# Edge ordering of a four-layer graph network: the one-hots laid down in four sub-blocks of four columns

## The chip, the cores and the metric

The kernel runs on one core of one Trainium2 chip. The metric is the device time of one launch, in microseconds (us), from all inputs in HBM to the output in HBM; lower is better. The engines are TensorE (PE in the profile; PEld is its weight load), VectorE (DVE), ScalarE (ACT), GpSimd (POOL) and SyncE (SP), which only issues transfers here.

## The reference, cut to what matters

Four message-passing layers over 6250 nodes and 200000 edges, with a residual sum and a layer norm after each.

```python
edge_index = jnp.stack([src, dst])
deg = jnp.maximum(jax.ops.segment_sum(jnp.ones(dst.shape, jnp.float32), dst, num_segments=6250), 1.0)
...
x = _layernorm(x + _L0_gnn_ref(x, deg_isqrt[:, None], L0_gnn_weight, L0_gnn_bias, src, dst), axis=-1)
x = _layernorm(x + _L1_gnn_ref(x, L1_gnn_w_neigh, L1_gnn_w_self, L1_gnn_b_self, src, dst), axis=-1)
x = _layernorm(x + _L2_gnn_ref(x, edge_index, L2_gnn_W1, ...), axis=-1)
x = _layernorm(x + _L3_gnn_ref(x, edge_index, L3_gnn_W1, ...), axis=-1)
```

Each layer gathers rows by `src` and sums them by `dst` (or the other way round). The edges come sorted by `dst`; the kernel first sorts them by tile of `src` as well, so that all later stages work on whole 128x128 or 128x512 pieces. The change touches this sorting alone, and nothing of the layers.

## The kernel before, in words

`program` runs its steps one after the other. A step ends with a barrier of all engines, so a step that ends earlier moves all later steps up by as much. `sort_edges` is the first step. It lays the edges down as 98 blocks (`BLOCKS`) of `K` = 16 columns of 128 edges, and has four parts: `load_columns`, `rank_columns` (the place of each edge in its block), `permute_columns` (each edge's record to its place, and the degrees), `bucket_ranges`.

`permute_columns` is where the change lies. For each block `n` (buffer half `h` = `n % 2`), the engines do this:

- VectorE (L386 to L391) makes five fp16 tiles. `lane` compares the 16 columns' lane numbers with a ramp of 64 values: 64x16 = 1024 elements in each partition. `row` does so with 128 values: 2048 elements. `dlo` does it for the last four columns: 128x4 = 512 elements. `piece` is `lane` times the high part and `lane` times the low part of the payload: 1024 elements each. In all of them the column is the innermost index, so the elements of one column are 16 elements, 32 bytes, apart (in `dlo`: four elements, 8 bytes). Before it starts it waits for `s_used`, which TensorE raises at the end of block `n - 2`. After every second block it also makes seven tiles of `high` for the next segment of 14 blocks (L396); in the last segment it doesn't.
- ScalarE (L443) makes `step`, 12 tiles of 128 elements in each partition, one for each of the first twelve columns (`steps(n + 1, ...)`, which waits for `s_used` too), and then takes block `n`'s sums out of PSUM (`results`, L448 and L449), once TensorE has summed them and the transfer of block `n - 2` has landed (`s_put`).
- TensorE sums the 16 columns in PSUM (L478): the stationary operand is `row[:, h, :, k]`, 128 columns wide, the moving one `piece[:, h, :, :, k]`, 128 columns wide, both read with a step of 32 bytes. Then come four matmuls for `dlo` (L481) and twelve for `step` (L484), each with a contiguous or 8-byte stationary operand and a moving operand `high` of 49 columns whose step is 448 bytes. `dlo` and `step` keep their forms under the change, and `high` does.
- GpSimd (L418, L421) adds the two parts and sends 128 records to HBM by an indirect transfer that accumulates.

```python
for k in range(K):
    put = nc.tensor.matmul(ps[:, h, 0:2 * LANES], row[:, h, :, k], piece[:, h, :, :, k].rearrange("p a l -> p (a l)"), start=k == 0, stop=k == K - 1)
put.then_inc(s_full, 1)
for k in range(OWN, K):
    nc.tensor.matmul(psh[:, 0:NT], dlo[:, h, :, k - OWN], tile_of(k), start=False, stop=False)
pe.wait_ge(s_step, n + 1)
for k in range(OWN):
    ins = nc.tensor.matmul(psd[:, 0:NT], step[:, h, k, :], tile_of(k), start=False, stop=False)
ins.then_inc(s_used, 1)
```

Of the kernel before, what the change touches and what calls it, by code (L numbers as in the profile page):

```python
# [5 lines left out]
F16 = mybir.dt.float16  # L6
# [3 lines left out]
ALU = mybir.AluOpType  # L10
# [3 lines left out]
P = 128  # L14
# [3 lines left out]
NT = -(-N_NODES // P)  # L18
# [2 lines left out]
CJ = 13  # L21
SCP = CJ * P
K = 16
LANES = 64
BLOCKS = -(-N_EDGES // (P * K))
CC = BLOCKS * K
# [38 lines left out]
def load_columns(nc, m, src, dst):  # L65
# [5 lines left out]
    with ExitStack() as ctx:  # L71
        sb = lambda n, s, d: ctx.enter_context(nc.sbuf_tensor(n, s, d))
# [24 lines left out]
        @block.gpsimd  # L97
        def _(gp):
            ch = Chain(gp, s_const)
            nc.gpsimd.memset(m.ones[:, :], 1.0).then_inc(s_const, 1)  # L100
            nc.gpsimd.iota(m.iota512[:, :], pattern=[[1, DB]], base=0, channel_multiplier=0, allow_small_or_imprecise_dtypes=True).then_inc(s_const, 1)
            nc.gpsimd.iota(m.iota128[:, :], pattern=[[1, P]], base=0, channel_multiplier=0, allow_small_or_imprecise_dtypes=True).then_inc(s_const, 1)
            nc.gpsimd.iota(m.row_id[:, :], pattern=[[0, 1]], base=0, channel_multiplier=1, allow_small_or_imprecise_dtypes=True).then_inc(s_const, 1)
            nc.gpsimd.iota(m.ramp[:, :, :], pattern=[[1, P], [0, K]], base=0, channel_multiplier=0, allow_small_or_imprecise_dtypes=True).then_inc(s_const, 1)
            ch.n = 5
            ch(nc.gpsimd.memset(m.zeros16[:, :], 0.0))
            ch(nc.gpsimd.affine_select(out=m.ident[:, :], in_=m.ones[:, :], compare_op=ALU.is_equal, fill=0.0, base=0, pattern=[[1, P]], channel_multiplier=-1))
            ch(nc.gpsimd.affine_select(out=m.before[:, :], in_=m.ones[:, :], compare_op=ALU.is_gt, fill=0.0, base=0, pattern=[[1, P]], channel_multiplier=-1))
            ch(nc.gpsimd.affine_select(out=m.shift1[:, :], in_=m.ones[:, :], compare_op=ALU.is_equal, fill=0.0, base=-1, pattern=[[1, P]], channel_multiplier=-1))
            ch(nc.gpsimd.affine_select(out=corner[:, :], in_=m.ones[:, :], compare_op=ALU.is_equal, fill=0.0, base=P - 1, pattern=[[1, P]], channel_multiplier=-1))  # L110
            nc.gpsimd.memset(zero[:, :], 0.0).then_inc(s_zero, 1)
# [229 lines left out]
def permute_columns(nc, m):  # L341


    OWN = 12
    SUB = 14
    SUBS = BLOCKS // SUB
    PAIRS = SUB // 2
    assert SUBS % 2 == 1 and NT % PAIRS == 0
    with ExitStack() as ctx:
        sb = lambda n, s, d: ctx.enter_context(nc.sbuf_tensor(n, s, d))  # L350
        sem = lambda n: nc.alloc_semaphore("pm_" + n)
        lane = sb("lane_hot", [P, 2, LANES, K], F16)
        piece = sb("piece_hot", [P, 2, 2, LANES, K], F16)
        row = sb("row_hot", [P, 2, P, K], F16)
        step = sb("dst_step", [P, 2, OWN, P], F16)
        dlo = sb("dst_low_hot", [P, 2, P, K - OWN], F16)
        high = sb("dst_tile_hot", [P, 2, NT, SUB * K], F16)
# [12 lines left out]

        @block.vector
        def _(dve):
            spread_over = lambda t, c, n, k: t[:, bass.ds(c, k)].unsqueeze(1).broadcast_to([P, n, k])
            for t in range(NT):
                ins = nc.vector.tensor_scalar(high[:, 0, t, :], m.dst_hi[:, 0:SUB * K], float(t), None, ALU.is_equal)
                if t % PAIRS == PAIRS - 1:
                    ins.then_inc(s_high, 1)

            def segment(s, turn, more=True):

                with dve.Fori(0, PAIRS) as i:
                    for h in (0, 1):
                        n = s * SUB + i * 2 + h
                        c = n * K
                        dve.wait_ge(s_used, n + 1)
                        nc.vector.tensor_tensor(lane[:, h, :, :], spread_over(m.lane, c, LANES, K), m.ramp[:, 0:LANES, :], ALU.is_equal).then_inc(s_lane, 1)  # L386
                        nc.vector.tensor_tensor(row[:, h, :, :], spread_over(m.rowkey, c, P, K), m.ramp[:, :, :], ALU.is_equal)
                        nc.vector.tensor_tensor(dlo[:, h, :, :], spread_over(m.dst_lo, c + OWN, P, K - OWN), m.ramp[:, :, 0:K - OWN], ALU.is_equal)
                        dve.wait_ge(s_lane, n + 1)
                        nc.vector.tensor_tensor(piece[:, h, 0, :, :], lane[:, h, :, :], spread_over(m.part1, c, LANES, K), ALU.mult)  # L390
                        nc.vector.tensor_tensor(piece[:, h, 1, :, :], lane[:, h, :, :], spread_over(m.part2, c, LANES, K), ALU.mult).then_inc(s_hot, 1)  # L391

                    if more:
                        for k in range(NT // PAIRS):
                            t = i * (NT // PAIRS) + k
                            ins = nc.vector.tensor_scalar(high[:, 1 - turn, bass.ds(t, 1), :].rearrange("p o w -> p (o w)"), m.dst_hi[:, bass.ds((s + 1) * (SUB * K), SUB * K)],  # L396
                                                          m.iota128[:, bass.ds(t, 1)], None, ALU.is_equal)
                        ins.then_inc(s_high, 1)

            with dve.Fori(0, SUBS // 2) as j:  # L400
                for turn in (0, 1):
                    segment(j * 2 + turn, turn)
            segment(SUBS - 1, 0, more=False)
            ch = Chain(dve, s_v)
            dve.wait_ge(s_counts, 1)

            ch(nc.vector.tensor_copy(si[:, :], psd[:, 0:NT]))
            ch(nc.vector.tensor_scalar(si[:, :], si[:, :], 1023, None, ALU.bitwise_and))
            ch(nc.vector.tensor_copy(sl[:, :], si[:, :]))
            nc.vector.tensor_tensor(sh[:, :], psd[:, 0:NT], sl[:, :], ALU.subtract).then_inc(s_parts, 1)  # L410
            ch(nc.vector.tensor_copy(counted[:, :], psh[:, 0:NT]))
            dve.wait_ge(s_deg, 1)
            ch(nc.vector.tensor_tensor(m.deg[:, :], counted[:, :], psd[:, 128:128 + NT], ALU.add))
# [47 lines left out]
        @block.tensor  # L461
        def _(pe):
            pe.sem_inc(s_used, 2)  # L463
            for p in (psd, psh):
                nc.tensor.matmul(p[:, 0:NT], m.zeros16[:, 0:P], m.zeros16[:, 0:NT], start=True, stop=False)

            def segment(s, turn):

                pe.wait_ge(s_high, (s + 1) * PAIRS)
                pe.sem_inc(s_begun_pe, 1)  # L470
                with pe.Fori(0, PAIRS) as i:
                    for h in (0, 1):
                        n = s * SUB + i * 2 + h
                        tile_of = lambda k: high[:, turn, :, bass.ds(i * (2 * K) + (h * K + k), 1)].rearrange("p t o -> p (t o)")
                        pe.wait_ge(s_both, n + 1)
                        pe.wait_ge(s_hot, n + 1)
                        for k in range(K):
                            put = nc.tensor.matmul(ps[:, h, 0:2 * LANES], row[:, h, :, k], piece[:, h, :, :, k].rearrange("p a l -> p (a l)"), start=k == 0, stop=k == K - 1)  # L478
                        put.then_inc(s_full, 1)
                        for k in range(OWN, K):  # L480
                            nc.tensor.matmul(psh[:, 0:NT], dlo[:, h, :, k - OWN], tile_of(k), start=False, stop=False)  # L481
# [5 lines that stand above are left out]
            with pe.Fori(0, SUBS // 2) as j:  # L487
                for turn in (0, 1):
                    segment(j * 2 + turn, turn)
            segment(SUBS - 1, 0)  # L490
            nc.tensor.matmul(psh[:, 0:8], m.zeros16[:, 0:P], m.zeros16[:, 0:8], start=False, stop=True)
            nc.tensor.matmul(psd[:, 0:8], m.zeros16[:, 0:P], m.zeros16[:, 0:8], start=False, stop=True).then_inc(s_counts, 1)
            pe.wait_ge(s_parts, 1)
            nc.tensor.matmul(psd[:, 128:128 + NT], m.steps[:, :], sl[:, :], start=True, stop=False)
            nc.tensor.matmul(psd[:, 128:128 + NT], m.steps[:, :], sh[:, :], start=False, stop=True).then_inc(s_deg, 1)
# [326 lines left out]
def sort_edges(nc, m, src, dst):  # L822
    with ExitStack() as ctx:
# [7 lines left out]
        m.before16 = sb("before16", [P, P], F16)  # L831
        m.shift1 = sb("shift_one", [P, P], F32)
        m.row_id = sb("row_id", [P, 1], F32)
        m.ramp = sb("ramp", [P, P, K], F16)
        m.tile_axis = sb("tile_axis", [P, NT], F16)
        m.tile_axis2 = sb("tile_axis2", [P, 161], F16)
        m.rowkey = sb("row_in_block", [P, SCP], F16)
# [1188 lines left out]
```

## Time and profile before

| | |
|---|---|
| time, median of 3 runs | 5341.95 us (5327.29 to 5349.08) |
| time of the profiled execution | 5343.12 us |
| its span, from first to last instruction | 5341.4 us |
| PE / PEld / DVE / ACT / POOL busy | 78% / 54% / 60% / 40% / 25% |
| mean granted TensorE clock | 0.81 of full speed |

The profiled execution's time is 1.7 us above its span and 1.2 us above the median. The span has long serial stages, each with a bound of its own; the busy shares over the whole of it say little about one stage. `permute_columns` is the stretch from about 236 to 760 us. The clock is given as a share of 2.4 GHz: 0.50 is 1.2 GHz. Instructions of an engine overlap at their ends, so the pace of a row of equal instructions is the distance of their starts, and less than the duration of one.

### The profile page before, as it was taken

How to read it: one execution, taken by the hardware profiler on the slowest of the kernel's cores; microseconds unless marked ns; L12 is line 12 of the kernel's file. 1: busy time of each engine (PE TensorE's matmuls, PEld its weight loads, DVE VectorE, ACT ScalarE, POOL GpSimd, SP SyncE). 2: the span in 40 equal slices, each digit the busy share in tenths (PEclk: the TensorE clock that was granted, in tenths of full speed). 3: DMA queues.
4: the chain of work that ended last, by engine and by line, in shares of the span. 5: the costliest groups of instructions: out<-in, count | busy, mean ns of one | idle time of the engine just before them, and what ended most of it. 6: DMA issues, size and time to landing. Idle time of an engine off the chain costs nothing. (4 is left out here: it accounts for less than half of the span.)

```text
span 5341.4 us, 100012 instructions
## 1 busy us (share of the span) xinstructions
PE 4157.3 (78%) x22671; PEld 2876.0 (54%) x22672; DVE 3223.2 (60%) x13041; ACT 2114.0 (40%) x6547; POOL 1339.9 (25%) x1340
## 2 busy tenths in 40 slices
PE   5699972799899997796996777777777777777772
PEld 2377752233344443344444667667677666677672
DVE  8877765998888887103004556555565555555565
ACT  0177750466788886102003333333333333333330
POOL 0043320000000000002001544444444444444440
PEclk8755555899999999897997788887888778887885
DMA  0011111001122221782872333333333333333330
GB/s 25 1 7 6 6 17 39 21 40 65 70 84 97 91 98 71 258 304 100 320 271 62 98 94 97 94 91 95 93 97 98 90 92 94 94 94 94 94 82 24
DMA packets 229819, 490.12 MB, mean 92 GB/s; under 512 B 51977, under 2 KB 146208, under 8 KB 229392
## 3 DMA queue, kind: packets, MB, share of 16 engines
q1 hardware_dynamic: 163269, 342.17, 19.1%
q0 software_dynamic: 66336, 145.89, 10.0%
q14 instruction: 177, 1.45, 0.1%
q8 instruction: 37, 0.61, 0.0%
HBM read 388.92 MB, written 99.01 MB: 91 GB/s over the span
## 5 line engine op out<-in xcount | busy, mean ns | idle before, releaser
L1681 POOL DMA_INDIRECT ea_gathered<-edge_table,ea_row_stage x1088 | 1070.2, 984 | 1198.4 <-DVE ea_row_stage L1736 610.1
L1763 DVE TENSOR_TENSOR agg_t<-agg_t,ea_psa 128x129 f32 x1632 | 461.9, 283 | 914.4 <-PE ea_psa L1850 502.4
L1827 PE MATMUL ea_psz<-parts,ea_onehot_t 128*128 x3264 | 709.0, 348 | 197.8 <-issue 179.0
L1827 PEld LDWEIGHTS ea_psz<-parts,ea_onehot_t 128*128 128x128 f32 x3264 | 605.9, 256 | 265.8 <-issue 265.2
L1144 PE MATMUL a_agg_ps<-a_adj_ring,parts 128*128 128x512 f16 (+1 forms) x2548 | 523.0, 369 | 45.3 <-DMA a_adj_ring<-adjacency 45.3
L1884 ACT ACTIVATE slot_dst<-ea_onehot,ea_mask 128x128 f32<-128x128 f16 x1632 | 535.3, 399 | 13.2
L942 PE MATMUL ab_agg_ps<-ab_adj_stage,parts 128*128 128x512 f16 x1911 | 535.1, 391 | 0.0
L443 ACT ACTIVATE dst_step<-iota,dst_low_bias 128x128 f16<-128x128 f16 x1188 | 358.4, 389 | 308.5 <-PEq L463 214.0
L1850 PE MATMUL ea_psa<-ea_near_x,slot_dst 128*128 128x129 f32 x1088 | 257.3, 324 | 277.3 <-issue 271.6
L1850 PE MATMUL ea_psa<-ea_gathered,slot_dst 128*128 128x129 f32 x2176 | 416.8, 353 | 68.7 <-DVE agg_t L1763 54.8
L1878 ACT ACTIVATE ea_mask<-ea_dot,b 128x4 f32<-128x4 f32 x408 | 121.3, 297 | 819.4 <-issue 423.6
L1850 PEld LDWEIGHTS ea_psa<-ea_gathered,slot_dst 128*128 128x128 f32 x2176 | 394.6, 270 | 77.1 <-DVE agg_t L1763 59.5
L1144 PEld LDWEIGHTS a_agg_ps<-a_adj_ring,parts 128*128 128x128 f16 x2548 | 242.0, 98 | 326.4 <-DMA a_adj_ring<-adjacency 45.8
L1015 ACT ACTIVATE ab_src_off<-iota,ab_neg_src 128x128 f16<-128x128 f16 x712 | 282.2, 396 | 300.6 <-PE ab_adj_ps L963 144.4
L478 PE MATMUL perm_ps<-piece_hot,row_hot 128*128 128x128 f16 x1568 | 392.6, 421 | 9.3 <-DVE piece_hot L391 9.3
L909 DVE TENSOR_SCALAR ab_dst_hot_middle<-iota,slot_dst 128x512 f16<-128x512 f16 x1218 | 391.9, 345 | 0.0
L1050 ACT ACTIVATE ab_adj_stage<-ab_adj_ps 128x512 f16<-128x512 f32 x637 | 372.2, 604 | 21.2 <-PE ab_adj_ps L968 19.3
L1876 ACT ACTIVATE ea_near_x<-ea_psx 128x512 f32<-128x512 f32 x136 | 81.2, 597 | 692.5 <-PE ea_psa L1850 375.5
L1850 PEld LDWEIGHTS ea_psa<-ea_near_x,slot_dst 128*128 128x128 f32 x1088 | 183.9, 217 | 315.6 <-issue 312.7
L963 PE MATMUL ab_adj_ps<-ab_dst_hot_middle,ab_src_hot_middle 128*128 128x512 f16 x1218 | 342.2, 384 | 11.6
L1831 PE MATMUL ea_psz<-v,ea_onehot_near 128*128 x2176 | 338.9, 279 | 0.0
L1379 POOL TENSOR_TENSOR parts<-xs,parts 128x896 f16<-128x896 f32 x7 | 13.2, 1882 | 1284.3 <-ACT parts L1373 1284.3
(381 smaller groups left out, 6854.1 us busy)
## 6 DMA issues: line engine op xcount, KB each, us to landing
a_adj_ring<-adjacency SPq DMA_DIRECT2D x182, 896.0 KB, 4.6
ea_low_rows<-low_rows SPq DMA_DIRECT2D x411, 128.0 KB
adjacency<-ab_adj_stage SPq DMA_DIRECT2D x91, 512.0 KB, 2.7
adjacency<-ab_adj_stage SPq DMA_DIRECT2D x91, 384.0 KB, 2.3
ea_near_rows<-near_rows SPq DMA_DIRECT2D x137, 128.0 KB
ea_gathered<-edge_table,ea_row_stage POOLq DMA_INDIRECT x1088
edge_table<-xs SPq DMA_DIRECT2D x12, 256.0 KB, 2.3
edge_table<-v SPq DMA_DIRECT2D x12, 256.0 KB, 2.8
```

Source lines behind the costliest of these rows:

```text
L443: ins = nc.scalar.activation(step[:, h, k, :], m.iota128h[:, :], ACT.Sign, bias=m.lo_bias[:, bass.ds(n * K + k, 1)])
L478: put = nc.tensor.matmul(ps[:, h, 0:2 * LANES], row[:, h, :, k], piece[:, h, :, :, k].rearrange("p a l -> p (a l)"), start=k == 0, stop=k ...
L909: return nc.vector.tensor_scalar(dst[:, k, :], m.iota512[:, :], float(t * SPAN), m.slot_dst[:, bass.ds(c, 1)], ALU.add, ALU.is_equal)
L942: ins = nc.tensor.matmul(agg_ps[:, :], lhs(r, t), stage[:, k, :], start=start and r == 0, stop=stop and r == parts - 1)
L963: nc.tensor.matmul(ps[:, k, :], src_m[:, k, :], dst_m[:, k, :], start=False, stop=False).then_inc(s_used_m[k], 1)
L1050: nc.scalar.activation(stage[:, k, :], ps[:, k, :], ACT.Copy, accum_out=col(m.out_deg, n * TG + k)).then_inc(s_taken[k], 1)
L1144: ins = nc.tensor.matmul(ps[:, h, 0:width], lhs(r, t), ring[:, g % SLOTS, k * DB:k * DB + width], start=t == 0 and r == 0, stop=t == NT - ...
L1681: nc.gpsimd.indirect_dma_start(got[:, h, g, k, 0:ROW], None, m.table, bass.IndirectOffsetOnAxis(ap=row_s[:, h, g, k:k + 1], axis=0)).then_ ...
L1763: ins = nc.vector.tensor_tensor(dst, dst, psa[:, home, k, 0:AW], ALU.add)
L1827: ins = nc.tensor.matmul(out, hot_t[:, g, k, :], of(m.u, tile_at(tiles[k])), start=True, stop=g != NEARBY)
L1850: ins = nc.tensor.matmul(psa[:, home, k, 0:AW], hot_m[:, g, k, :], what, start=True, stop=True)
L1884: ins = nc.scalar.activation(hot_m[:, g, k, :], hot[:, h, g, :, k], ACT.Copy, scale=mask[:, g, k:k + 1])
```

## The change

`Q` = 4 is new. The tiles `lane`, `piece` and `row` get an outer index of `K // Q` = 4 sub-blocks, and within a sub-block the column (of four) is innermost. The elements of one column of a block are then four elements, 8 bytes, apart, in each of these tiles. VectorE writes the same number of elements with the same number of instructions; its operand of per-column values is now read as 4 sub-blocks x (repeated 64 or 128 times) x 4 columns, and the ramp, which has four equal elements for each value and no more sixteen, is read again for each sub-block. The ramp that GpSimd makes once (L104) has 512 elements in each partition, before 2048.

```diff
+Q = 4
...
-            nc.gpsimd.iota(m.ramp[:, :, :], pattern=[[1, P], [0, K]], base=0, channel_multiplier=0, allow_small_or_imprecise_dtypes=True).then_inc(s_const, 1)
+            nc.gpsimd.iota(m.ramp[:, :, :], pattern=[[1, P], [0, Q]], base=0, channel_multiplier=0, allow_small_or_imprecise_dtypes=True).then_inc(s_const, 1)
...
-        lane = sb("lane_hot", [P, 2, LANES, K], F16)
-        piece = sb("piece_hot", [P, 2, 2, LANES, K], F16)
-        row = sb("row_hot", [P, 2, P, K], F16)
+        lane = sb("lane_hot", [P, 2, KQ, LANES, Q], F16)
+        piece = sb("piece_hot", [P, 2, KQ, 2, LANES, Q], F16)
+        row = sb("row_hot", [P, 2, KQ, P, Q], F16)
...
-            spread_over = lambda t, c, n, k: t[:, bass.ds(c, k)].unsqueeze(1).broadcast_to([P, n, k])
+            spread_over = lambda t, c, n: t[:, bass.ds(c, K)].rearrange("p (a q) -> p a q", q=Q).unsqueeze(2).broadcast_to([P, KQ, n, Q])
+            ramps = lambda n: m.ramp[:, 0:n, :].unsqueeze(1).broadcast_to([P, KQ, n, Q])
...
-                        nc.vector.tensor_tensor(lane[:, h, :, :], spread_over(m.lane, c, LANES, K), m.ramp[:, 0:LANES, :], ALU.is_equal).then_inc(s_lane, 1)
-                        nc.vector.tensor_tensor(row[:, h, :, :], spread_over(m.rowkey, c, P, K), m.ramp[:, :, :], ALU.is_equal)
-                        nc.vector.tensor_tensor(dlo[:, h, :, :], spread_over(m.dst_lo, c + OWN, P, K - OWN), m.ramp[:, :, 0:K - OWN], ALU.is_equal)
+                        nc.vector.tensor_tensor(lane[:, h, :, :, :], spread_over(m.lane, c, LANES), ramps(LANES), ALU.is_equal).then_inc(s_lane, 1)
+                        nc.vector.tensor_tensor(row[:, h, :, :, :], spread_over(m.rowkey, c, P), ramps(P), ALU.is_equal)
+                        nc.vector.tensor_tensor(dlo[:, h, :, :], m.dst_lo[:, bass.ds(c + OWN, Q)].unsqueeze(1).broadcast_to([P, P, Q]), m.ramp[:, :, :], ALU.is_equal)
...
-                        nc.vector.tensor_tensor(piece[:, h, 0, :, :], lane[:, h, :, :], spread_over(m.part1, c, LANES, K), ALU.mult)
-                        nc.vector.tensor_tensor(piece[:, h, 1, :, :], lane[:, h, :, :], spread_over(m.part2, c, LANES, K), ALU.mult).then_inc(s_hot, 1)
+                        nc.vector.tensor_tensor(piece[:, h, :, 0, :, :], lane[:, h, :, :, :], spread_over(m.part1, c, LANES), ALU.mult)
+                        nc.vector.tensor_tensor(piece[:, h, :, 1, :, :], lane[:, h, :, :, :], spread_over(m.part2, c, LANES), ALU.mult).then_inc(s_hot, 1)
...
-                            put = nc.tensor.matmul(ps[:, h, 0:2 * LANES], row[:, h, :, k], piece[:, h, :, :, k].rearrange("p a l -> p (a l)"), start=k == 0, stop=k == K - 1)
+                            put = nc.tensor.matmul(ps[:, h, 0:2 * LANES], row[:, h, k // Q, :, k % Q], piece[:, h, k // Q, :, :, k % Q].rearrange("p a l -> p (a l)"), start=k == 0, stop=k == K - 1)
```

## Rows read from the trace of the kernel before

**Rows 1.** Busy time by engine in the stretch of the 98 blocks.

```profile
core 0: us, PE busy (x) PEld busy (x) DVE busy (x) ACT busy (x) POOL busy (x), PEclk, DMA share, GB/s
246.20:756.80 510.60, 510.53 (x3138) 365.55 (x3138) 381.54 (x779) 387.35 (x1360) 201.94 (x195) 0.50 0.11 6
```

**Rows 2.** Waits from 240 to 760 us: total us, times, longest.

```profile
DVE lane_hot L386 <- PE degree_ps L484: 122.1, 96, 1.9
ACT dst_step L443 <- PE degree_ps L484: 94.5, 97, 1.1
```

**Rows 3.** Timeline of two blocks: start us, us, what, count, idle time before.

```profile
501.02 0.35 POOL L418 TENSOR_TENSOR record_rows<-both_parts 128x64 f32<-128x64 f32 x1 [2.39 <-ACT both_parts L449]
501.41 4.00 PE L478 MATMUL perm_ps<-piece_hot,row_hot 128*128 128x128 f16 x16
502.17 1.70 POOL L421 DMA_INDIRECT records<-record_rows,record_row  x1 [0.80 <-POOL record_rows L418]
505.23 0.53 PE L481 MATMUL degree_hot_ps<-dst_tile_hot,dst_low_hot 128*128 x4
505.58 1.21 PE L484 MATMUL degree_ps<-dst_tile_hot,dst_step 128*128 x12
506.62 3.99 PE L478 MATMUL perm_ps<-piece_hot,row_hot 128*128 128x128 f16 x16
```

**Rows 4.** Weight loads by tile: ns min/median/max, first and last start.

```profile
L478 PEld LDWEIGHTS perm_ps<-piece_hot,row_hot x1568: 140/147/169, 246.2 to 754.7; 128*128 128x128 f16 x196
L481 PEld LDWEIGHTS degree_hot_ps<-dst_tile_hot,dst_low_hot x392: 122/127/132, 249.8 to 755.4; 128*128 128x128 f16 x196
L484 PEld LDWEIGHTS degree_ps<-dst_tile_hot,dst_step x1176: 121/124/126, 250.3 to 756.4; 128*128 128x128 f16 x196
```

**Rows 5.** Matmuls with contiguous fp16 operands: timeline, line, stretch (columns as above).

```profile
49.01 3.02 PE L306 MATMUL tile_count_ps<-tile_hot,tile_axis 128*113 128x416 f16 x8 [29.48 <-DVE tile_hot L221]
...
L306 PE MATMUL tile_count_ps<-tile_hot,tile_axis x196: 326/326/595, 49.0 to 159.6; 128*113 128x384 f16 x147, 128*113 128x416 f16 x49
...
49.00:51.50 2.50, 2.49 (x8) 1.59 (x9) 2.50 (x15) 0.00 (x0) 0.00 (x0) 0.50 0.00 0
```

**Rows 6.** VectorE's fp16 compares and products by line: ns min/median/max.

```profile
L386 DVE TENSOR_TENSOR lane_hot<-lane,ramp x98: 678/693/693, 242.7 to 746.5; 128x1024 f16<-128x1024 f16 x98
L387 DVE TENSOR_TENSOR row_hot<-row_in_block,ramp x98: 1211/1218/1221, 243.3 to 747.1; 128x2048 f16<-128x2048 f16 x98
L388 DVE TENSOR_TENSOR dst_low_hot<-dst_low,ramp x98: 411/418/424, 244.5 to 748.2; 128x512 f16<-128x512 f16 x98
L390 DVE TENSOR_TENSOR piece_hot<-lane_hot,payload_high x98: 678/684/687, 244.8 to 748.5; 128x1024 f16<-128x1024 f16 x98
L1743 DVE TENSOR_TENSOR ea_onehot<-ea_src_low,ea_ramp x411: 416/419/472, 2930.4 to 5196.2; 128x512 f16<-128x512 f16 x137
```

**Rows 7.** Timeline of the stage's start, where neither engine waits for TensorE.

```profile
236.63 7.12 ACT L443 ACTIVATE dst_step<-iota,dst_low_bias 128x128 f16<-128x128 f16 x24 [214.02 <-PEq L463]
...
246.02 0.68 DVE L386 TENSOR_TENSOR lane_hot<-lane,ramp 128x1024 f16<-128x1024 f16 x1
...
249.29 1.39 DVE L396 TENSOR_SCALAR dst_tile_hot<-dst_tile,iota  x7
```

**Rows 8.** Last block: timeline, GpSimd's sends by line, stretches.

```profile
755.54 0.20 ACT L448 ACTIVATE record_row<-block_rows 128x1 int32 x1 [0.25 <-PE perm_ps L478]
755.65 0.26 ACT L449 ACTIVATE both_parts<-perm_ps 128x128 f32<-128x128 f32 x1
...
L421 POOL DMA_INDIRECT records<-record_rows,record_row x78: 1670/1783/2090, 299.0 to 700.0; - x78
...
758.90:760.40 1.50, 0.00 (x0) 0.00 (x0) 0.21 (x1) 0.00 (x0) 0.00 (x0) 0.50 0.39 22
760.40:766.00 5.60, 0.00 (x0) 0.00 (x0) 0.00 (x0) 0.00 (x0) 0.00 (x0) 0.50 0.00 0
```

**Rows 9.** Timeline of the kernel's first microseconds, GpSimd.

```profile
1.87 2.46 POOL L104 IOTA ramp<- 128x2048 f16 x1
```

More of the change, by code:

```diff
@@ L347, in permute_columns @@
     PAIRS = SUB // 2
-    assert SUBS % 2 == 1 and NT % PAIRS == 0
+    KQ = K // Q
+    assert K - OWN == Q and SUBS % 2 == 1 and NT % PAIRS == 0
     with ExitStack() as ctx:
@@ L833, in sort_edges @@
         m.row_id = sb("row_id", [P, 1], F32)
-        m.ramp = sb("ramp", [P, P, K], F16)
+        m.ramp = sb("ramp", [P, P, Q], F16)
         m.tile_axis = sb("tile_axis", [P, NT], F16)
```

## The prediction

> **What bounds the kernel now.** I first asked in which stretch the touched lines run, and took the busy time of the engines there [rows 1]. From 246.2 to 756.8 us TensorE is busy for 510.5 of 510.6 us; VectorE is busy for 382 and ScalarE for 387. So this stage is bound by TensorE and by nothing else, and the granted clock is 0.50 all through it, the lower of the two levels (1.2 GHz). Next the list of waits [rows 2]: VectorE waits 122 us in 96 places and ScalarE 94 us in 97 for the last matmul of a block (L484). Nothing on TensorE's side waits in return. Then the timeline of two blocks, for the pace [rows 3]. The sum matmuls of two blocks following each other start at 501.41 and 506.62, so a block is 5.21 us. Of that the 16 sum matmuls (L478) take 505.23 - 501.41 = 3.82 us, 239 ns each; the four of L481 take 0.35 us, 87 ns each; the twelve of L484 take 1.04 us, 87 ns each. With 97 such distances between the first and the last block the stage's body is 97 x 5.21 = 505 us. That is what can be shortened. All other stages are untouched and follow behind a barrier, so what the stage gives comes off the total at full value.
>
> **What a sum matmul would cost.** The rows give the price of a column at this clock from both sides. Contiguous: eight matmuls of 416 columns run from first start to last end in 3.02 us, the last alone 0.595, so one follows the other after 2.425 / 7 = 346 ns, or 0.83 ns a column, which is one cycle of 1.2 GHz; the granted clock there is 0.50 too [rows 5]. With a step of 448 bytes: 87 ns for 49 columns, 1.77 ns a column. With 32 bytes: 239 ns for 128 columns, 1.87 ns a column. So beyond some step a moving column costs two cycles and not one. For 128 columns two cycles are 213 ns, which leaves 26 ns of 239; for 49 columns they are 82 ns, which leaves 5 of 87. The rest goes with the stationary operand: its load takes 147 ns in L478 (32-byte step), 127 ns in L481 (8 bytes) and 124 ns in L484 (contiguous) [rows 4]. Loads are pulled under the matmul before, and what shows of one is about its duration less 120 ns: 27, 7 and 4.
>
> The new form has an 8-byte step on both sides. The stationary side is measured: L481's load has exactly this step and costs 3 ns more than a contiguous one, against 23 ns for 32 bytes [rows 4]. No row of before has a moving operand with an 8-byte step. Its bounds are one cycle and two cycles a column: 107 + 7 = 114 ns, or 213 + 7 = 220 ns. I take 114, because the weight load reads the same memory from the same engine and shows that 8 bytes are nearly free where 32 are not. A block of TensorE is then 16 x 0.114 + 0.35 + 1.04 = 3.21 us in place of 5.21; with the other bound 4.91.
>
> The Trainium skill speaks to just this. Its page "SBUF — State Buffer" (the box on cachelines) says that the memory has lines of 16 bytes and that two accesses have to fall in a line for full rate. By it an 8-byte step is free: the 3.21 us. Its page "Vector Engine (DVE) Microarchitecture Reference", section 5.2, says of VectorE's ports that only runs of two adjacent 4-byte words stream at full rate, and that a hop at every element costs about 0.65 cycle. If TensorE's port were like that, a column would cost 1.65 cycles, a sum matmul about 183 ns and a block 4.3 us; that is one of the rivals below. This trace agrees with the first page for the weight load, and shows nothing for the moving operand.
>
> **Who sets the pace then.** TensorE at 3.21 us falls behind two others, so not all of the 2.0 us can come back.
>
> VectorE: one block of its five instructions runs from 246.02 to 249.29, 3.27 us, where it waits for nobody, and L396's seven tiles, once in two blocks, take seven distances of (1.39 - 0.27) / 6 = 0.187 us, 1.31 us [rows 7]. That is (2 x 3.27 + 1.31) / 2 = 3.93 us a block in the 84 blocks that have L396, and 3.27 in the last 14. The elements are as many as before. The operands are not quite as before: they come in runs of four elements, where most had 16 or more. The rows have that case: `dlo` (L388) reads its ramp in runs of four 32 bytes apart and its other operand as four elements over and over, and takes 418 ns for 512 elements; L387 takes 1218 for 2048 and L390 684 for 1024 [rows 6]. From 512 to 1024 that is 0.52 ns an element, from 1024 to 2048 it is also 0.52: short runs cost nothing. What no row has is an fp16 operand with three indices, sub-block, repeat, column. The bounds are nothing and a fall from two elements a cycle to one. I take nothing, the side on which L388 and L1743 lie; the other is a rival.
>
> ScalarE: 24 instructions L443 without a wait take 7.12 us, so twelve take 12 x (7.12 - 0.39) / 23 = 3.51 us [rows 7]; the two of `results` take from 755.54 to 755.91, 0.37 us [rows 8]. That is 3.88 us with nothing overlapped. It has to start `steps` of a block after TensorE has ended the one two before, and `results` after the sums; at 3.21 us a block TensorE is early for both.
>
> GpSimd: a send takes 502.17 - 501.02 = 1.15 us from the start of the adding (L418) to that of the issue [rows 3], and the issue (L421) 1.78 us in the median [rows 8]: 2.93 us. A block's parts are ready at 755.91 and the transfer is over by 760.4, when the DMA share drops to nought [rows 8]: 4.5 us. ScalarE asks for it two blocks later, now 10.4 us, then 7.9. It stays hidden with 3.4 us to spare. L396 and L421 will more often run side by side on VectorE and GpSimd; L1743 runs beside such sends for most of the last stage and its median of 419 ns is L388's 418 [rows 6], so I charge nothing.
>
> So VectorE leads with 3.93 and ScalarE follows at 3.88. Two engines that close, coupled through two buffer halves and with L396 coming in pairs, will lose a little to each other; I take 3.98 us (bounds 3.93 and 4.25). In the last segment ScalarE leads: 3.8.
>
> **The sum.** 83 x (5.21 - 3.98) = 102.1 us; 14 x (5.21 - 3.80) = 19.7 us; the last block has no follower and its sums are 16 x (0.239 - 0.114) = 2.0 us shorter. Together 124 us. The ramp (L104) [rows 9] shrinks from 2.46 us to a quarter, about 1.8 us less, but it lies in the first 2 to 5 us, where the loads of the edges are under way and end later; it counts nothing, at most 1.8 us either way. The profiled execution took 5343.1 us, so 5343 - 124 = 5219 us; the median of the runs shown lies 1.2 us lower, which makes 5218. I say 5220. The clock adds nothing: at the upper level TensorE would be still earlier, and it isn't the bound any more; if it stays at 0.50, as in the 510 us where it was never idle, the sum holds as it stands.
>
> **Rivals.**
> 1. The 8-byte step still costs part or all of the second cycle on the moving operand. TensorE stays the bound as soon as a sum matmul costs over (3.98 - 1.39) / 16 = 0.162 us. At 183 ns a block is 4.32: 97 x 0.89 = 86 us saved, 5257 us. At the full 220 ns it is 4.91: 29 us saved, 5314 us. For it: no row has such a moving operand. Against it: the weight load. 0.09.
> 2. VectorE takes the three-index operands at one element a cycle. The four changed instructions have 5120 elements, and 0.52 ns more for each is 2.65 us: 5.92 us a block, 6.58 with L396. The stage is 84 x 6.58 + 14 x 5.92 = 636 us in place of 511: 125 us slower, 5468 us. This is the case on the other side, and it decides from 5.21 us a block on: if the elements cost over (5.21 - 3.93) / 5120 = 0.25 ns more, half as much again as now. L388's short runs speak against it; nothing shows three indices. 0.06.
> 3. The coupling is worse than I think: ScalarE's and VectorE's waits for L484 add up in turn. With 4.25 us a block 97 x 0.96 = 93 us are saved, 5250 us. 0.10; it lies inside my range.
> 4. Nothing comes of it, because another wait (the landing of the records, the handing out of TensorE's instructions with an address computed for each `high` column) holds a block at 5.2 us: 5340 us. TensorE's instructions follow each other without a gap now, so a second bound at the same height would be chance. 0.03.
>
> My own case has 0.72.
>
> **Range and chances.** The likeliest case, 3.93 to 4.1 us, with some 8 us for the spread of runs, gives 5206 to 5240. The case 3 and the 183 ns of case 1 carry it to 5262. What lies outside is the dear end of case 1, cases 2 and 4 and the unforeseen, under 0.2. No change from noise is told apart here within 0.5%, 27 us. Cases 1 and 3 and mine are faster by more than that, the dearest end of 1 just so: 0.90. Within: 0.04. Slower, by case 2: 0.06.
>
> **What would show it.** In the stretch of the 98 blocks TensorE's busy share falls below those of VectorE and ScalarE, and the starts of L478 within a block are 114 ns apart (between 107 and 120); the weight load of L478 has a median near 127 ns; the distance between blocks is 3.9 to 4.1 us; VectorE is busy for over 95%, with L386 to L391 at their old durations; the wait of L386 for L484 is gone or a few microseconds in all, and L478 waits for L391 instead. `bucket_ranges` starts near 643 us and no more at 767. I am wrong if L478's starts are over 160 ns apart, or if L387 takes well over 1218 ns.

## The result and the profile after

The changed kernel takes 5272.39 us in the median of six runs (5267.45 to 5286.02), against 5334.59 us in six runs of the kernel before (5307.15 to 5349.08). The ratio is 0.9891, with a 95% interval from 0.9865 to 0.9917. So 62 us came off, where 124 had been forecast, and 5272 lies above the range. The profiled execution took 5269.35 us (span 5267.6).

The line numbers of the changed kernel are those of before plus three: L478 became L481, L386 became L389, L418 became L421. First the groups by line, with ns minimum, median and maximum, to be held against [rows 4, 6, 8]:

```profile
L481 PEld LDWEIGHTS perm_ps<-piece_hot,row_hot x1568: 110/124/139, 246.0 to 694.5; 128*128 128x128 f16 x196
L389 DVE TENSOR_TENSOR lane_hot<-lane,ramp x98: 673/680/764, 242.5 to 689.2; 128x1024 f16<-128x1024 f16 x98
L390 DVE TENSOR_TENSOR row_hot<-row_in_block,ramp x98: 1207/1214/1337, 243.1 to 689.9; 128x2048 f16<-128x2048 f16 x98
L393 DVE TENSOR_TENSOR piece_hot<-lane_hot,payload_high x98: 675/679/828, 244.6 to 691.3; 128x1024 f16<-128x1024 f16 x98
L394 DVE TENSOR_TENSOR piece_hot<-lane_hot,payload_low x98: 675/690/911, 245.2 to 691.9; 128x1024 f16<-128x1024 f16 x98
L421 POOL TENSOR_TENSOR record_rows<-both_parts x98: 308/698/6205, 248.6 to 699.0; 128x64 f32<-128x64 f32 x98
L424 POOL DMA_INDIRECT records<-record_rows,record_row x98: 1555/1557/1937, 250.3 to 700.1; - x98
```

The weight load is down from 147 to 124 ns. VectorE's instructions kept their medians in spite of three indices; only single ones are longer (L390 up to 1337 ns, L394 up to 911). One row is out of order: GpSimd's addition of 64 values. It took 0.35 us in the block shown of before [rows 3] and 0.37 at most in all 98, and now takes up to 6.2.

Then the block starts, as timeline rows of the first, the 85th and the 98th block:

```profile
246.05 1.22 PE L481 MATMUL perm_ps<-piece_hot,row_hot 128*128 128x128 f16 x9 [9.35 <-DVE piece_hot L394]
...
642.04 2.05 PE L481 MATMUL perm_ps<-piece_hot,row_hot 128*128 128x128 f16 x16 [1.20 <-DVE piece_hot L394]
...
692.88 2.05 PE L481 MATMUL perm_ps<-piece_hot,row_hot 128*128 128x128 f16 x16
```

That is (642.04 - 246.05) / 84 = 4.71 us a block where `high` is rebuilt (L399), and (692.88 - 642.04) / 13 = 3.91 us where it is not. Before it was 5.21 [rows 3], in the one stretch as in the other. The busy times of the stretch and its largest waits (us, times, longest) stand against [rows 1, 2]:

```profile
246.00:692.80 446.80, 346.45 (x3104) 320.79 (x3104) 387.71 (x779) 363.12 (x1338) 316.82 (x191) 0.50 0.13 7
```

```profile
ACT record_row L451 <- DMA records<-record_rows,record_row: 78.1, 22, 5.2
...
DVE lane_hot L389 <- PE degree_ps L487: 56.4, 30, 5.9
...
PE perm_ps L481 <- ACT both_parts L452: 40.7, 21, 3.8
PE perm_ps L481 <- DVE piece_hot L394: 35.1, 25, 9.4
```

TensorE fell from 100% busy to 78%, and the clock stayed at 0.50. But VectorE, which was to lead, is at 388 of 447 us, 87%. Nobody is full. And a wait has appeared that the list of before does not have at all: ScalarE stands 78 us, in 22 places, until the records of two blocks ago have landed. The timeline of one such place:

```profile
449.61 1.21 DVE L390 TENSOR_TENSOR row_hot<-row_in_block,ramp 128x2048 f16<-128x2048 f16 x1
449.62 6.20 POOL L421 TENSOR_TENSOR record_rows<-both_parts 128x64 f32<-128x64 f32 x1 [1.05 <-ACT both_parts L452]
...
454.96 0.68 DVE L394 TENSOR_TENSOR piece_hot<-lane_hot,payload_low 128x1024 f16<-128x1024 f16 x1
455.56 1.46 DVE L399 TENSOR_SCALAR dst_tile_hot<-dst_tile,iota  x7
...
456.61 1.65 POOL L424 DMA_INDIRECT records<-record_rows,record_row  x1 [0.79 <-POOL record_rows L421]
...
457.74 6.02 POOL L421 TENSOR_TENSOR record_rows<-both_parts 128x64 f32<-128x64 f32 x1
...
459.89 0.20 ACT L451 ACTIVATE record_row<-block_rows 128x1 int32 x1 [3.27 <-DMA records<-record_rows,record_row]
...
460.45 1.82 PE L481 MATMUL perm_ps<-piece_hot,row_hot 128*128 128x128 f16 x14 [1.23 <-DVE piece_hot L394]
```

From 449 us VectorE runs two-operand instructions back to back, and the addition that starts at 449.62 ends at 455.82. That is 0.26 us after VectorE has come to L399, the tensor-scalar comparisons, which read one tensor. The next one ends at 463.76, and its L399 starts at 463.50 on VectorE: 0.26 us again. The first record lands at 459.89, 10.3 us after its addition began; ScalarE had been asking for 3.3 us. Its `results` come late, TensorE's next sums with them, and VectorE then waits for TensorE.

Not every addition fares so. 22 of the 98 take 3.8 to 6.2 us: 21 of them end when the tiles of L399 have begun, one when VectorE has run out of work. But 41 others, which also begin beside a two-operand instruction with another following at once, end some 0.26 us after the start of that next one. One of the last blocks shows it:

```profile
687.55 0.68 DVE L393 TENSOR_TENSOR piece_hot<-lane_hot,payload_high 128x1024 f16<-128x1024 f16 x1
687.77 0.64 POOL L421 TENSOR_TENSOR record_rows<-both_parts 128x64 f32<-128x64 f32 x1 [0.78 <-ACT both_parts L452]
688.16 0.81 DVE L394 TENSOR_TENSOR piece_hot<-lane_hot,payload_low 128x1024 f16<-128x1024 f16 x1
```

The addition ends at 688.41, and L394 takes 0.81 us in place of 0.68. What decides between the two cases no run shows. In this kernel 21 of the 22 long ones began within the first 0.21 us of L390, and all but one of those that began in it from 0.38 us on got in at the next instruction.

The Trainium skill has this rule ("SBUF — State Buffer", section "Who interferes with whom"): VectorE and GpSimd share one pair of ports, a VectorE instruction with two inputs from this memory takes it, and a GpSimd instruction that reads the memory has to wait, and the other way round. The trace agrees on the culprits, and in the 41 short cases on the length too. In the 22 long ones it doesn't, if the rule is read as a wait for one instruction: those of 6.0 to 6.2 us last over nine that follow each other.

### The profile page after: what moved, and what is told of

Same layout as the page of the kernel before. It is cut to its first block and busy times, and to the rows that moved or that the text cites. A ratio compares the mean times of both kernels' runs of the same rounds, so it can differ in the third digit from the quotient of the medians.

```text
span 5267.6 us, 100012 instructions
## 1 busy us (share of the span) xinstructions
PE 3975.3 (75%) x22671; PEld 2824.4 (54%) x22672; DVE 3230.7 (61%) x13041; ACT 2095.0 (40%) x6547; POOL 1460.8 (28%) x1340
## 3 DMA queue, kind: packets, MB, share of 16 engines
q0 software_dynamic: 66336, 145.89, 10.3%
## 5 line engine op out<-in xcount | busy, mean ns | idle before, releaser
L1830 PE MATMUL ea_psz<-parts,ea_onehot_t 128*128 x3264 | 720.7, 349 | 245.0 <-issue 226.3
L1853 PE MATMUL ea_psa<-ea_near_x,slot_dst 128*128 128x129 f32 x1088 | 235.8, 311 | 251.1 <-issue 247.4
L945 PEld LDWEIGHTS ab_agg_ps<-ab_adj_stage,parts 128*128 128x128 bf16 x1911 | 190.7, 100 | 229.9 <-issue 20.9
```

The source lines that it names most:

```text
L945: ins = nc.tensor.matmul(agg_ps[:, :], lhs(r, t), stage[:, k, :], start=start and r == 0, stop=stop and r == parts - 1)
L1830: ins = nc.tensor.matmul(out, hot_t[:, g, k, :], of(m.u, tile_at(tiles[k])), start=True, stop=g != NEARBY)
L1853: ins = nc.tensor.matmul(psa[:, home, k, 0:AW], hot_m[:, g, k, :], what, start=True, stop=True)
```

## The experiments

All nine kernels carry one common edit: in three loops of a later stage the lower bound is `smax(begin, 0)`. The first was run to see that this changes nothing of substance.

**1. Control: the changed kernel with that edit.**

```diff
-                        with dve.Fori(begin, end) as i:
+                        with dve.Fori(smax(begin, 0), end) as i:
```

> A control. The changed kernel, with the lower bounds of three loops of the adjacency build clamped to nought, which every further kernel here has too. The ordering stage is untouched: all theories expect 4.6 us a block there as in the changed kernel (4.71 in the first 84 blocks, 3.91 in the last), 98 adds of GpSimd of which the longest are 6.0 to 6.2 us, and a total within 15 us of the changed kernel's 5272 us. It shows what the clamps cost elsewhere.

It took 5326.83 us in a single run against 5386.97 for before on the same chip, 0.989, with blocks of 4.67 and 3.90 us. The blocks are as expected; the total is 55 us above the changed kernel's 5272, on a chip where the kernel before takes 52 us more as well. So totals are compared within one chip only: experiments 1 to 4 ran on this one. The control stands for the changed kernel in 2 to 4.

**2. GpSimd's addition taken away.** The two parts are summed in PSUM instead, by 32 matmuls of 64 columns in place of 16 of 128, and ScalarE writes the records' rows itself.

```diff
-                nc.gpsimd.tensor_tensor(rec[:, h, :], both[:, h, 0, :], both[:, h, 1, :], ALU.add).then_inc(s_added, 1)
-                gp.wait_ge(s_added, n + 1)
...
-                nc.scalar.activation(both[:, h, :, :].rearrange("p a l -> p (a l)"), ps[:, h, 0:2 * LANES], ACT.Copy, scale=float(P)).then_inc(s_both, 1)
+                nc.scalar.activation(rec[:, h, :], ps[:, h, 0:LANES], ACT.Copy, scale=float(P)).then_inc(s_both, 1)
...
+                            for a in (0, 1):
+                                put = nc.tensor.matmul(ps[:, h, 0:LANES], row[:, h, k // Q, :, k % Q], piece[:, h, k // Q, a, :, k % Q], start=k == 0 and a == 0, stop=k == K - 1 and a == 1)
```

> GpSimd's add of the two parts is gone: TensorE sums both parts into the same 64 columns of PSUM, in 32 matmuls of 64 columns in place of 16 of 128, and ScalarE writes the record straight away. Theory A (GpSimd's add stands still while VectorE runs its two-input compares and products back to back, and the late send holds up ScalarE and then TensorE): no instruction of GpSimd reads its operands beside VectorE any more, the block falls to 3.95 to 4.1 us, VectorE is busy for over 95% of the stage, and the total is some 60 us under the changed kernel, 5205 to 5220 us. Theory B (VectorE and ScalarE, with 3.93 and 3.88 us a block nearly equal, lose time to each other through the two buffer halves, or the transfers themselves land late): the add was not the cause, the block stays at 4.5 to 4.7 us and the total at 5265 to 5280. TensorE has 32 x about 62 ns in place of 16 x 117, some 0.1 us more a block, under the other engines' time in both theories.

5306.95 us, ratio to before 0.9846 (0.9823 to 0.987), blocks of 4.49 and 3.78 us. That is 0.18 us a block better than the control in the first 84, a quarter of the 0.7 that is missing. The addition is gone, and the stall is not. It now sits on the issue of the indirect transfer:

```profile
L422 POOL DMA_INDIRECT records<-record_rows,record_row x98: 1552/1922/7632, 249.7 to 679.0; - x98
```

```profile
437.11 7.63 POOL L422 DMA_INDIRECT records<-record_rows,record_row  x1 [0.30 <-issue]
...
446.56 0.20 ACT L449 ACTIVATE record_row<-block_rows 128x1 int32 x1 [4.16 <-DMA records<-record_rows,record_row]
```

It begins beside two-operand work and ends at 444.74, 1.51 us after VectorE came to its one-operand tiles (L399, at 443.23): about the 1.55 us of the shortest issues. The pace lies where theory B had it (4.5 to 4.7) and misses theory A's 3.95 to 4.1. So my first wording of the theory, which blamed the addition alone, was too narrow.

**3. The train cut in two.** The tiles of `high` (L399) are the only one-operand instructions of VectorE here, and all seven stand after every second block. I put three of them after the first block of a pair and four after the second. The first three need a further wait for TensorE.

```diff
+                        if more and h == 0:
+                            dve.wait_ge(s_used, n + 2)
-                    if more:
-                        for k in range(NT // PAIRS):
+                        for k in ((0, 1, 2), (3, 4, 5, 6))[h] if more else ():
```

> GpSimd's add stays. VectorE's seven one-input tiles of the next segment are made in two parts, three after the first block of a pair and four after the second, where all seven came after the second, with one wait more (for the block before) ahead of the three. VectorE's work is the same. Theory A: GpSimd gets an opening after every block and not after every other, so no add lasts over about 3.4 us (one block of VectorE's two-input instructions) in place of 6.2; the sends come in time, and the block falls from 4.71 to 4.0 to 4.2 us; total 5210 to 5235. Theory B: the same work in another order, and one wait more; 4.6 to 4.8 us a block, total 5265 to 5285.

5274.1 us, ratio 0.9787 (0.9764 to 0.981), blocks of 4.13 and 3.82 us. No work was taken away, and a wait was added, yet the block of the first 84 fell by 0.54 us. The addition's longest is now 1.85 us, and VectorE is at 377 of 380 us, 99%:

```profile
L424 POOL TENSOR_TENSOR record_rows<-both_parts x98: 308/1022/1846, 249.3 to 649.0; 128x64 f32<-128x64 f32 x98
L427 POOL DMA_INDIRECT records<-record_rows,record_row x98: 1555/1728/7829, 251.5 to 650.1; - x98
```

```profile
250.00:630.00 380.00, 319.06 (x2966) 300.77 (x2965) 377.28 (x755) 356.51 (x1289) 284.73 (x184) 0.50 0.14 8
```

ScalarE's wait for the records fell from 75 us in the control to 3.5. Theory A had forecast 4.0 to 4.2 us a block and no addition over 3.4 us, and both came. The stall is not gone: 21 of the 98 issues now take over 3 us, up to 7.83. But ScalarE waits for only two records in the whole stage.

**4. Both together.**

> Both edits together. Theory A: with the add gone the openings are worth nothing, and the wait that comes with them can only cost: 3.95 to 4.1 us a block, as with the add gone alone, total 5205 to 5225. Theory B: 4.5 to 4.8 us a block, total 5265 to 5285.

5263.58 us, ratio 0.9772 (0.9746 to 0.9798), blocks of 3.98 and 3.77 us: the lowest median of the study.

```profile
L424 POOL DMA_INDIRECT records<-record_rows,record_row x98: 1552/3571/7004, 250.3 to 637.2; - x98
```

The issues are still stalled, 56 of them for over 3 us, but hardly anyone waits for them any more: ScalarE 3.0 us in all. With the addition gone, what is left of the path fits into the two blocks that it has. The expectation was wrong on one point: it gave the openings no worth once the addition was gone, and they brought the block from 4.49 to 3.98 us.

**5. and 6. The stall without the change.** If two-operand work on VectorE is enough, the kernel before must show the stall once its VectorE is filled up. Both kernels are the kernel before with spare work that nobody reads: one with two comparisons of two tensors a block, the other with one reduction of one tensor of the same total length, 1.21 us.

```diff
+                        for j in (0, 1):
+                            nc.vector.tensor_tensor(spare[:, h, j, :].rearrange("p (l k) -> p l k", k=K), m.ramp[:, 0:LANES, :], m.ramp[:, LANES:P, :], ALU.is_equal)
```

> The kernel before (32-byte steps, a block of 5.21 us set by TensorE), with two spare compares of two inputs (1024 elements each, 1.2 us together) after VectorE's products of each block, into a tile that nobody reads. VectorE then has 3.93 + 1.21 = 5.14 us of work a block. Theory A, in the wider form that the last runs call for (whatever GpSimd does with its port of the memory, the add or the issue of the send, stands still under VectorE's two-input instructions): GpSimd's adds of 0.31 us grow to several us, up to 9, the sends come late, and the block rises to 5.5 us or more, with the step of 32 bytes untouched. Theory B (nearly equal engines lose time to each other through the two halves): VectorE and TensorE are nearly equal now, so the block rises too, by some tenths, but the adds keep their 0.31 us.

```diff
+                        nc.vector.tensor_reduce(spare[:, h, 0, 0:1], m.ramp[:, 0:LANES, :].rearrange("p l k -> p (l k)"), AX.X, ALU.max)
```

> The same, with one spare instruction of one input (a maximum over 1024 elements, about 1.15 us) in the place of the two compares. VectorE is as busy as with those. Theory A: one-input work leaves GpSimd its port, the adds stay within about 0.3 to 1.2 us and the block at 5.2 to 5.3 us. Theory B: the same rise as with the two compares, since VectorE's time is the same.

Against 5326.08 us of before on their chip, two operands took 5377.35 us and one operand 5322.58, a single run each. The blocks took 5.49 and 5.21 us (first 84; in the last 13 both 5.21). So 24 of the 51 us lie in the blocks, and the reading rests on these; the rest is no more than single runs of one kernel differ. The groups and VectorE's busy time from 300 to 640 us, two operands first:

```profile
L422 POOL TENSOR_TENSOR record_rows<-both_parts x98: 310/926/8427, 251.5 to 780.8; 128x64 f32<-128x64 f32 x98
...
322.06 3.95 POOL L422 TENSOR_TENSOR record_rows<-both_parts 128x64 f32<-128x64 f32 x1
...
325.75 0.80 DVE L388 TENSOR_TENSOR lane_hot<-lane,ramp 128x1024 f16<-128x1024 f16 x1
...
396.52 8.43 POOL L422 TENSOR_TENSOR record_rows<-both_parts 128x64 f32<-128x64 f32 x1
...
404.69 1.46 DVE L400 TENSOR_SCALAR dst_tile_hot<-dst_tile,iota  x7
...
300.00:640.00 340.00, 327.38 (x1994) 232.84 (x1993) 330.74 (x653) 245.13 (x872) 245.18 (x124) 0.50 0.10 6
```

```profile
L421 POOL TENSOR_TENSOR record_rows<-both_parts x98: 307/312/1249, 250.8 to 756.2; 128x64 f32<-128x64 f32 x98
...
300.00:640.00 340.00, 340.00 (x2088) 243.23 (x2087) 337.63 (x624) 260.79 (x916) 191.50 (x131) 0.50 0.11 6
```

VectorE is as full in the one as in the other, even a little fuller with one operand. With two operands 89 of the 98 additions overlap a two-operand instruction and the longest takes 8.43 us; it ends at 404.95, once more 0.26 us after the one-operand tiles start. With one operand 77 overlap none, because the spare reduction stands where they fall, and the longest takes 1.25 us. With one operand a full VectorE costs nothing, though it makes its seven tiles of `high` in one go as well. So the cause is neither that the engines are nearly equal nor that these tiles come together, but the kind of instruction beside the send. A run of one kind is not the whole rule of its length, though: the addition at 322.06 waits over five two-operand instructions and is then done 0.26 us after the start of L388, which is of the same kind and follows without a pause.

**7. to 9. Which side's step the price hangs on.** Three kernels, one run each: only the stationary operand in sub-blocks of four columns; only the moving one; and both in sub-blocks of eight, a step of 16 bytes. The side left alone keeps its old layout and a 16-wide ramp of its own, made once.

```diff
-                            put = nc.tensor.matmul(ps[:, h, 0:2 * LANES], row[:, h, :, k], piece[:, h, :, :, k].rearrange("p a l -> p (a l)"), start=k == 0, stop=k == K - 1)
+                            put = nc.tensor.matmul(ps[:, h, 0:2 * LANES], row[:, h, k // Q, :, k % Q], piece[:, h, :, :, k].rearrange("p a l -> p (a l)"), start=k == 0, stop=k == K - 1)
```

> The changed kernel with only the stationary side (row) at an 8-byte step; lane and piece keep 32 bytes, and VectorE's shapes for them those of before. By the prediction's split of a sum matmul (213 ns of two-cycle columns, and the load's excess of 27 ns with 32 bytes or 7 with 8) L482's starts are 220 ns apart; TensorE is the bound with 16 x 0.220 + 1.39 = 4.91 us a block. If only the two together matter, or the excess of 27 ns has another cause, it is 235 to 240 ns and 5.2 us.

```diff
-                            put = nc.tensor.matmul(ps[:, h, 0:2 * LANES], row[:, h, :, k], piece[:, h, :, :, k].rearrange("p a l -> p (a l)"), start=k == 0, stop=k == K - 1)
+                            put = nc.tensor.matmul(ps[:, h, 0:2 * LANES], row[:, h, :, k], piece[:, h, k // Q, :, :, k % Q].rearrange("p a l -> p (a l)"), start=k == 0, stop=k == K - 1)
```

> The changed kernel with only the moving side (lane, piece) at an 8-byte step; row keeps 32 bytes. By the same split a sum matmul is 107 + 27 = 134 ns, 3.53 us a block for TensorE, under VectorE's 3.93: the block is as slow as in the changed kernel, 4.5 to 4.8 us, for GpSimd's sake (theory A), with adds of up to 6.2 us. If the load's excess doesn't add to a one-cycle matmul, the starts are 117 ns apart.

```diff
-Q = 4
+Q = 8
+R = 4
```

> The changed kernel with two sub-blocks of eight columns in place of four of four: the elements of a column are 16 bytes apart on both sides. It asks where the second cycle of a moving column comes in, between 8 bytes (118 ns a sum matmul) and 32 (240 ns). The Trainium skill, page 'SBUF - State Buffer', box on cachelines, has lines of 16 bytes with two accesses in a line wanted: by it 16 bytes are as dear as 32, 213 ns and the rest, 230 to 240 ns, and the block is back at 5.1 to 5.2 us under TensorE. If the cost begins beyond 16 bytes, the starts are 118 ns apart and the block is the changed kernel's 4.6 us. VectorE's instructions keep their durations in both cases.

| | moving step | stationary step | sum matmul, ns | load, ns | block, first 84 / last 13 |
|---|---|---|---|---|---|
| before | 32 B | 32 B | 240 | 147 | 5.21 / 5.21 |
| stationary only | 32 B | 8 B | 233 | 126 | 5.12 / 5.12 |
| both sides, Q = 8 | 16 B | 16 B | 234 | 145 | 5.12 / 5.12 |
| moving only | 8 B | 32 B | 121 | 146 | 4.72 / 3.91 |
| changed kernel | 8 B | 8 B | 118 | 124 | 4.71 / 3.91 |

The first two took 5323.79 and 5268.77 us against 5326.08 of before. The third took 4494.76 against 4498.63; on that chip a later stage, which both kernels share, is some 830 us shorter (the granted clock in the third kernel's trace is 0.98 from 2900 us on, against 0.81 in the first one's), and only the stage of the blocks is read from it. The row for 16 bytes, sixteen sum matmuls and their successors:

```profile
405.52 3.92 PE L483 MATMUL perm_ps<-piece_hot,row_hot 128*128 128x128 f16 x16
409.25 0.53 PE L486 MATMUL degree_hot_ps<-dst_tile_hot,dst_low_hot 128*128 x4
```

(409.25 - 405.52) / 16 = 233 ns. So the second cycle of a column is there at 16 bytes in full and not at 8, and nearly all of the change's effect is the moving side. The expectations had 220 ns and 4.91 us a block for the stationary side alone, and 134 ns for the moving one alone; 233, 5.12 and 121 were measured, near the second value that each of them gave. With the moving side alone the sends stall as in the changed kernel (the addition's longest 6.26 us); with the two that leave TensorE the bound, the longest is 0.34 us.

## Why the prediction was half right

**The sum matmul: right.** Forecast 114 ns, measured 118, within the 107 to 120 given. The working behind it was right in total only. It put 20 of the 126 ns on the stationary operand; the two single-sided kernels give that side 3 to 7 ns and the moving side 115 to 119. The argument from the weight load to the moving operand held for 8 bytes, but it was an analogy: at 16 bytes the load takes 145 ns and the matmul its full second cycle, so there the two do agree.

**Rival 1, the 8-byte step still dear: refuted**, with 118 ns in place of 183 or 220. **Rival 2, three indices at one element a cycle: refuted**, with 1214 ns for 2048 elements, where 1218 were measured before. **Rival 4, another wait at 5.2 us: not seen.** **Rival 3, a pace of 4.25 us from coupling**, was right that waits between the engines would grow, but too small (4.71) and wrong on the cause: ScalarE's and VectorE's waits for TensorE are results of a late record. With the train cut in two the same engines, coupled as before and with one wait more, run at 4.13 us, and without the addition at 3.98, the forecast number. What coupling by itself costs is therefore at most 0.2 us over VectorE's 3.93.

**The step that failed** is the one that costed GpSimd: "It stays hidden with 3.4 us to spare", and of L396 and L421 side by side "I charge nothing". Two things were wrong in it. The durations of a send were taken from a stage in which VectorE paused at every block for TensorE [rows 2], 1.27 us on the average. In before, no addition overlaps a two-operand instruction at all: 57 begin in such a pause, 41 beside L396. The one shown in [rows 3] runs from 501.02 to 501.37:

```profile
499.80 1.40 DVE L396 TENSOR_SCALAR dst_tile_hot<-dst_tile,iota  x7
501.74 0.69 DVE L386 TENSOR_TENSOR lane_hot<-lane,ramp 128x1024 f16<-128x1024 f16 x1 [0.54 <-PE degree_ps L484]
```

The change removes most of the pauses, so the duration was no constant of the work. And the cover was looked up for the issue beside one-operand tiles and for L1743's own duration [rows 6], that is, whether VectorE suffers. It doesn't; GpSimd does. The addition went from 0.31 us to up to 6.2, the send from 4.5 us to over 10, past the 7.9 us it had.

**The sum with that term.** The first 84 blocks lost 84 x (4.71 - 3.98) = 61 us of the forecast and the last 13 lost 13 x (3.91 - 3.80) = 1.4 us. That is nearly 63 of the 67 us that the stage fell short: `bucket_ranges` starts at 709.99 us in place of 767.15, which is 57 us and not 124. Another 3 us are at the last block. Its sums were to be 2.0 us shorter and were, but ScalarE, which leads there, took them out only 5.5 us after the block's start, at 698.38 (4.2 before [rows 8]), so nothing came of it and the tail from the block's start on grew from 15.8 to 17.1 us. The rest is rounding. That the loss is confined to the first 84 fits the cause: there a train of VectorE runs through two blocks, ten instructions in 6.5 us. In the last 14 VectorE needs 3.27 us of 3.91 and pauses in every block, and no addition takes over 1.02 us.

**Of the signs named beforehand,** the matmuls' distance, the weight load, VectorE's old durations and L478's new wait for VectorE (35 us in 25 places) came. VectorE above 95%, 3.9 to 4.1 us a block, `bucket_ranges` near 643 and only "a few microseconds" of L386's wait for L484 (56 us were measured) did not in the first 84. The stage's 57 us and the medians' 62 differ by less than the runs of either kernel do among themselves.

## What to carry to other kernels

A duration read from a trace holds for the neighbours it had there. When a change lets an engine run without pauses, ask which small instruction of another engine lived in those pauses; beside VectorE's two-operand work it was an addition on GpSimd here, and the issue of an indirect transfer. Where it can't be avoided, spread VectorE's one-operand instructions as breaks between the others, or give the send another buffer half's worth of time (which no run here tried); here the breaks alone were worth about 1% of the kernel, as much as the change itself.

## What the runs showed of the hardware

**GpSimd's wait can outlast one instruction of VectorE.** Its addition of 64 values a partition took 0.31 us alone, and up to 6.2, 6.3 and 8.4 us beside two-operand instructions of VectorE that followed each other without a pause. In three of the long cases shown it ended 0.26 us after the first instruction of another kind had started. But it can also get in between two of the same kind: 41 of the 98 additions of the changed kernel ended some 0.26 us after the start of the next two-operand instruction, and one of the filled kernel did so after 3.95 us. Which of the two happens is not explained here. The instructions of VectorE were little disturbed: the five of a block take 3.77 us together in the changed kernel and took 3.69 before, with a longest of 1337 ns (L390) and 911 (L394).

**The issue of an indirect transfer waits too,** up to 7.63 us with no addition beside it, up to 7.83 us in the kernel with the train cut in two, and up to 4.93 us in the kernel filled with one-operand work, in whose trains five two-operand instructions still stand. In the changed kernel it is undisturbed (1.56 us in the median, 1.94 at most); that the addition ahead of it takes the wait there is a reading that no run tests.

**TensorE's moving operand pays a second cycle for a column between 8 and 16 bytes of step,** at once and in full (121 and 233 ns for 128 columns at the 0.50 clock). The page "SBUF — State Buffer" of the Trainium skill, in its box on cachelines, asks for two accesses in each 16-byte line, and these runs agree. The same box adds that eight values of two bytes can be strided for free; that is a step of 16 bytes, and here it costs nearly all that 32 bytes cost (234 against 240 ns). The measurement decides: four values, 8 bytes. Steps between 8 and 16 bytes were not tried.
